# Transposing every second expert block by DMA in place of every third, and seeding before the transposing transfer is issued

## The reference

```python
# layer 1: masked linear
w_masked = weight * elem_mask            # 32x32 blocks of the mask
x = x + layernorm(x) @ w_masked.T
# layer 2: mixture of experts, 8 experts, top 2
h = layernorm(x)
_, top_idx = top_k(h @ W_gate + b_gate, 2)
y_all = relu(einsum('bsd,edh->bseh', h, W_e) + b_e)
x = x + take_along_axis(y_all, top_idx[..., None], axis=2).mean(axis=2)
```

## Time and profile before

| what | value |
|---|---|
| time, median of 3 runs | 684.41 us (682.28 to 686.14) |
| the profiled execution's own time | 682.73 us |
| its span in the profile | 681.0 us |
| PE busy | 661.3 us (97%) |
| DVE, ACT, POOL busy | 300.6, 338.0, 274.5 us (44%, 50%, 40%) |
| granted TensorE clock | 0.996 |
| experts' stage | from about 245 us to the end |

### The profile page before, as it was taken

One profiled execution on the slowest core, in us unless ns is written; L12 is line 12 of the kernel. 1 busy time (PEld: TensorE's weight loads), 2 busy tenths in 40 slices (PEclk: granted clock), 3 DMA queues, 4 the chain that ended last, 5 costly groups with the idle time before them and its releaser, 6 DMA issues.

```text
span 681.0 us, 11115 instructions
## 1 busy us (share of the span) xinstructions
PE 661.3 (97%) x3455; PEld 537.2 (79%) x3455; DVE 300.6 (44%) x559; ACT 338.0 (50%) x437; POOL 274.5 (40%) x254
## 2 busy tenths in 40 slices
PE   6999999999999999999999999999999999999993
PEld 4667777878888787888887888888888888888883
DVE  5886688887796645351440640441542420000000
ACT  6876855678784435343443435353535353535340
POOL 2023121235382454445362635362636353535231
PEclk9999999999999999999999999999999999999998
DMA  8991946699773499688699795787795966342423
GB/s 346 408 407 43 375 186 224 240 324 321 253 247 155 172 247 255 164 246 205 176 275 120 201 265 124 181 248 159 200 281 133 231 184 111 45 83 37 89 37 56
DMA packets 62165, 137.08 MB, mean 201 GB/s; under 512 B 30240, under 2 KB 30240, under 8 KB 62112
## 3 DMA queue, kind: packets, MB, share of 16 engines
q1 hardware_dynamic: 25776, 92.85, 37.7%
q0 software_dynamic: 11376, 37.23, 25.8%
q10 hardware_dynamic: 24960, 6.29, 6.3%
HBM read 87.59 MB, written 46.14 MB: 196 GB/s over the span
## 4 chain that ended last, share of the span: by engine, by line
PE 91%; DMA 3%; ACTq 1%; DVE 1%; ACT 1%; issue 1%; SPq 0%; POOLq 0%; POOL 0%
PE psO L491 80%; PE psT L781 3%; PE psT L491 2%; PE psT L524 2%; PE psO L524 1%; PE psG L597 1%; DMA xb<-data_t 1%; DMA x<-x_planes,tok_of 1%; DMA raw<-L_ffn_W_e 1%; ACTq L1096 1%; PE psS L578 1%; DVE slots L1397 1%; PE psT L565 0%; PE psT L609 0%; DVE slots L1395 0%
## 5 line engine op out<-in xcount | busy, mean ns | idle before, releaser
L491 PE MATMUL psO<-slots,xT 128*128 (+1 forms) x1872 | 432.8, 391 | 1.9 <-ACT psO L1056 1.5
L491 PEld LDWEIGHTS psO<-slots,xT 128*128 128x128 f32 x1872 | 349.2, 188 | 74.0 <-issue 2.6
L491 PE MATMUL psO<-wT,xT 128*128 128x512 f32 x624 | 152.3, 397 | 0.0
L1759 POOL DMA_INDIRECT rows_out<-xb,tok_of x36 | 61.1, 1697 | 209.4 <-ACT xb L1143 205.3
L1395 DVE CAST slots<-raw 128x1024 fp32r<-128x1024 f32 x56 | 56.6, 1010 | 190.3 <-PE psO L491 99.3
L1143 ACT ACTIVATE xb<-psO 128x512 f32<-128x512 f32 x78 | 46.6, 598 | 182.4 <-PE psO L491 182.4
L491 PEld LDWEIGHTS psO<-wT,xT 128*128 128x128 f32 x624 | 114.3, 188 | 25.1 <-issue 2.7
L1753 POOL TENSOR_TENSOR xT<-x2T,xT 128x1024 fp32r<-128x1024 f32 x38 | 94.6, 2490 | 16.6 <-ACT x2T L1119 14.4
L1056 ACT ACTIVATE psO<-bias_slot 128x512 f32 (+1 forms) x78 | 47.0, 602 | 76.9 <-issue 36.1
L1397 DVE TENSOR_TENSOR slots<-raw,slots 128x1024 fp32r<-128x1024 f32 x56 | 68.6, 1225 | 1.9
L1681 POOL TENSOR_SCALAR rs<-squares 128x1 f32<-128x1 f32 x16 | 8.8, 551 | 70.5 <-ACT rows_a L905 41.1
(11 more groups left out here) (238 smaller groups left out, 563.3 us busy)
## 6 DMA issues: line engine op xcount, KB each, us to landing
raw<-L_ffn_W_e SPq DMA_DIRECT2D x56, 512.0 KB, 5.1
x_rows<-x SPq DMA_DIRECT2D x16, 512.0 KB, 4.6
xb<-data_t SPq DMA_DIRECT2D x12, 512.0 KB, 4.3
mask_stage<-mask_blocks SPq DMA_DIRECT2D x8, 512.0 KB, 11.4
w_stage<-weight_t SPq DMA_DIRECT2D x8, 512.0 KB, 12.2
row_stage<-L_attn_weight SPq DMA_DIRECT2D x8, 512.0 KB, 10.7
xr<-L_attn_data SPq DMA_DIRECT2D x8, 512.0 KB, 5.8
x_planes<-planes_even SPq DMA_DIRECT2D x8, 512.0 KB, 3.0
```

The source lines that it names most:

```text
L491: last = eng.matmul(psum, xT[:, p, a, kt, :], moving(b, kt), start=(i == 0 and kt == 0 and not seeded), stop=(i == len(PASSES) - 1 and kt ...
L1759: eng.indirect_dma_start(out, bass.IndirectOffsetOnAxis(ap=tok_col(b), axis=0), xb[:, b % 2, :], None, bounds_check=N_TOK + P - 1, compute ...
```

## The change

Blocks 5, 7, ..., 37 go the DMA way (17 in place of 12), so `rows_of`, the gathers, POOL's order and ACT's joins follow from `by_dma`. On ACT the seed of half 0 of block b + 1 (with its two value loads) comes ahead of `turn_rows(b + 3)`; and a turn now waits for the join of the block two before it in place of three. DVE's table of how many turns must have landed ahead of a pair of weight loads is computed anew: a turn every four counts of `c_half` in place of every six, and never a turn that is issued behind the seed of the block for which those weights are wanted (`through - 2`); that takes four more small instructions.

```diff
@@ -315,7 +315,7 @@
         GATHER_AT = NB - 2
 
         def by_dma(b):
-            return b > EARLY + 2 and b % 3 == 2
+            return b > EARLY + 2 and b % 2 == 1
 
         def turns_of_pe(b):
             return len([c for c in range(1, b + 1) if not by_dma(c)])
@@ -324,7 +324,7 @@
             return len([c for c in range(1, b + 1) if by_dma(c)])
 
         N_TURNS = turns_of_dma(N_BLOCKS - 1)
-        assert [b for b in range(N_BLOCKS) if by_dma(b)] == list(range(5, 5 + 3 * N_TURNS, 3))
+        assert [b for b in range(N_BLOCKS) if by_dma(b)] == list(range(5, 5 + 2 * N_TURNS, 2))
 
         def turn_bank(b):
             return 0 if b == 0 else (b + 1) % 2
@@ -468,7 +468,7 @@
                     if kt % 2 == 0 and n > KT:
                         pair = n // 2 - 1
                         if n == KT + 2:
-                            eng.wait_ge(c_pace, KT // 2 + 4)
+                            eng.wait_ge(c_pace, KT + 4)
                         turned_by = after_turn[0:1, pair % (KT // 2), pair // (KT // 2) - 1:pair // (KT // 2)]
                         eng.wait_ge(l_turn, eng.value_load(turned_by, min_val=16, max_val=16 * (N_TURNS + 1)))
                     eng.dma_start(raw[:, kt % 2, :], w_rows(expert, kt)).then_inc(l_raw[kt % 2], 16)
@@ -1092,7 +1092,7 @@
                     eng.wait_ge(l_x1[2], 16 * uses_of(2, NB))
                     eng.wait_ge(c_ln2, NB)
                 else:
-                    eng.wait_ge(c_rhi, 2 * (b - 3))
+                    eng.wait_ge(c_rhi, 2 * (b - 2))
                 eng.dma_start_transpose(turned[:], rows_of(b).bitcast(U16)).then_inc(l_turn, 16)
 
             def join_rows(b):
@@ -1142,12 +1142,12 @@
                     eng.wait_ge(c_half, NH * (b + 1) + n + 1)
                     eng.activation(xb[:, b % 2, n * HALF:(n + 1) * HALF], psO[:, n, :], ACT.Relu,
                                    scale=1.0 / TOP_K).then_inc(c_out, 1)
-                    if n == 0 and b + 3 < N_BLOCKS and by_dma(b + 3):
-                        turn_rows(b + 3)
                     if b + 1 < N_BLOCKS:
                         if n == 0:
                             slot = biases_of(b + 1)
                         seed_half(b + 1, slot, n)
+                    if n == 0 and b + 3 < N_BLOCKS and by_dma(b + 3):
+                        turn_rows(b + 3)
                     if b == 1 and n == 0:
                         rows_hi(b + 1)
 
@@ -1615,12 +1615,16 @@
                 eng.scalar_tensor_tensor(pace[:, j, :], through[:, 0:N_EXP - 1], float(j), through[:, 1:N_EXP],
                                          ALU.add, ALU.min).then_inc(c_pace, 1)
             eng.wait_ge(c_pace, KT // 2)
-            eng.tensor_scalar(turn_part[:], pace[:], -1.0, 43.0, ALU.add, ALU.mult).then_inc(c_pace, 1)
-            eng.wait_ge(c_pace, KT // 2 + 1)
-            eng.tensor_scalar(turn_no[:], turn_part[:], 8, None, ALU.logical_shift_right).then_inc(c_pace, 1)
-            eng.wait_ge(c_pace, KT // 2 + 2)
+            for j in range(KT // 2):
+                eng.scalar_tensor_tensor(turn_no[:, j, :], through[:, 1:N_EXP], -2.0, pace[:, j, :],
+                                         ALU.add, ALU.min).then_inc(c_pace, 1)
+            eng.wait_ge(c_pace, KT)
+            eng.tensor_scalar(turn_part[:], turn_no[:], -3.0, None, ALU.add).then_inc(c_pace, 1)
+            eng.wait_ge(c_pace, KT + 1)
+            eng.tensor_scalar(turn_no[:], turn_part[:], 2, None, ALU.logical_shift_right).then_inc(c_pace, 1)
+            eng.wait_ge(c_pace, KT + 2)
             eng.tensor_scalar(turn_part[:], turn_no[:], float(N_TURNS), 1.0, ALU.min, ALU.add).then_inc(c_pace, 1)
-            eng.wait_ge(c_pace, KT // 2 + 3)
+            eng.wait_ge(c_pace, KT + 3)
             eng.tensor_scalar(after_turn[:], turn_part[:], 16.0, None, ALU.mult).then_inc(c_pace, 1)
             for e in range(2, N_EXP):
                 for kt in range(KT):
```

## The result

| | before | changed |
|---|---|---|
| median of 5 runs | 682.71 us (682.28 to 686.14) | 675.64 us (674.96 to 675.84) |
| span of the profiled execution | 681.0 us | 673.9 us |
| turns by DMA / by PE | 12 / 27 | 17 / 22 |

The ratio is 0.9885 (95% interval 0.9861 to 0.9908): 1.15% faster, where 0.94% was forecast. The medians differ by 7.07 us, which is 1.04%. Timed again (experiment 5), the changed kernel had 675.69 us beside 683.52, ratio 0.9881 (0.9863 to 0.9898).

A forecast was written before the change was run, and what follows sets the result against it. PE was taken to bound the kernel, so savings of 4.5 us (five fewer PE turns) and 1.9 us (seed gaps) summed to 6.4, from the 684.41 us median to 678.0 us, 0.9% faster; range 675.0 to 682.5 us.

The forecast's parts named there:

- part 2: Seed put ahead of the turn's issue on ACT: PE's three gaps vanish, 1.01 + 0.42 + 0.51 = 1.9 us saved.
- anchor: Starting time for the savings: median of three runs, 684.41 us, giving 678.0; the profiled execution, 682.73, gives 676.3.
- What bounds the kernel: PE, 97% busy over the 681.0 us span and 308.62 of 308.70 us in nearly the whole expert stage.
- part 1: Five blocks fewer turned by PE, 0.89 us each: 4.5 us saved, all on the path.
- The swap has to be there: With denser turns PE wants the seed about 4.6 us after the evacuation; the old order reaches 4.6 to 5.9.
- Part 3: Single buffers for gathered planes and turned rows, round 34.4 to 22.7 us: cost nothing, bounds 0 and 30 us.
- rival B: Late planes or a stretched turn hold ACT in two or three of 16 rounds: 680 to 683 us; chance 0.13.
- Rival C: The buffers' round bounds: denser turns and other transfers slow one another, 1.9 us per round, 708 us; chance 0.06.
- The 65% of the DMA engines: DMA engines' busy share in the expert-stage stretch, given as evidence against transfers slowing one another until the round bounds.
- Part 4: SP's holds of weight loads until turns land: three of 2.8 us don't reach the 16.22 us cover; cost nothing.
- 1309 ns for a tile by DMA: The skill's table, 390 ns on TensorE: as an estimate 20.9 us a turn and a loss; the trace's 5 us disagreed.

The follow-up runs named there:

- experiment 5: The changed kernel timed again with nothing altered, beside the kernel before: 675.69 us against 683.52.
- experiment 1: Kernel before with only the seed moved ahead of the turn's issue, plus the limit on weight-load holds this needs; turns every third block as before: 679.21 us, ratio 0.9947.
- Experiment 2: Changed kernel (every second block by DMA) with the old order, the turn's issue ahead of the seed: 684.93 us, ratio 1.0015.
- experiment 6: Changed kernel with two buffers each for gathered planes and turned rows, and two in place of three for the PE way: 675.2 us.
- f2: Changed kernel with two buffers of each kind and every block from 5 on turned by DMA (34 turns): 699.83 us, ratio 1.0207.
- experiment 4: Changed kernel without SP's wait for turns ahead of a pair of weight loads: 675.39 us, ratio 0.9891.
- g2: Changed kernel with SP holding a pair of weight loads already when the next turn is due within one half block: 674.93 us, ratio 0.9889.
- experiment 9: Changed kernel with two buffers of each kind and a dense tail, every block from 30 on turned by DMA: 670.22 us, ratio 0.9818.

## Why the prediction was right in kind, and what was off in size

The step that failed is the price of part 2. A late seed was priced at the matmul side's gaps, 1.9 us, and it cost what the weight-load side stood idle, 2.67 us. The median came out 2.4 us below the forecast, 675.64 and not 678.0; 1.7 of that are the anchor (below), and the 0.8 of this step account for the rest.

- **What bounds the kernel, and part 1**: right. The stretch from block 0 to block 38 lost 7.22 us, of which 2.67 are the order's (experiment 1), so 4.55 are the five turns, 0.91 each; the term was 4.5, with 0.89 each from a bare block rounded to 10.9 (it is 10.88).
- **Part 2** is the term that was mis-sized: 1.9 us, by adding up PE's idle brackets. By the periods between evacuations it cost 2.67. The list I read had the line for PEld, 2.6 us in three times, and I took the matmul side. Experiment 2 has the same at a longer stall: PE's gap is 2.54 us, the weight-load side's 2.77, and the block took 14.57 us in place of 11.79, 2.78 more. Why the two sides differ by a quarter of a microsecond isn't shown; the ends of matmuls are modelled in these profiles, so it may lie in the record of PE's gap.
- **The anchor** made it 678.0 rather than 676.3. The profiled execution (682.73) with the measured terms gives 682.73 - 7.2 = 675.5, and 675.64 came out; the median of the first three runs, 684.41, stood 1.7 above what five runs gave. That part of the miss is scatter.
- **The swap has to be there** (part 2's last sentences): right. Alone the denser turns gave nothing, 684.93 us. In the sum 4.5 and 1.9 stand as two gains, but the 4.5 come only with the swap.
- **Part 3** took the worst turn of one trace, 15 us, as the worst there is. 21 us came in an unchanged kernel, and 28 beside the first loads. Its verdict for the median, nothing, was right (experiment 6); rival B comes in 1 of the 11 runs of the changed kernel and costs 4 us, by one stall and not by two or three.
- **Rival C** was not this change's, but it starts not far behind: f2. The time is decided by single turns that meet other traffic and not by the mean round. The 65% of the DMA engines that stood against it was a mean over two stages: in the kernel before they are at 0.80 from 257 to 550 us, while weights are loaded, and at 0.42 behind, and the change made the first 0.88.
- **Part 4**: right about the cost of the holds (experiment 4), but not about their size. It took three of 2.8 us at most; the changed kernel has 29.4 us in six, the longest 8.4. The cover was real: the 47.8 us of holds in g2 cost PE 1.2 us, at one place.
- **The Trainium skill's** 1309 ns for a tile by DMA ("VectorE: DVE Perf Modes", "The three transpose paths") made 20.9 us of a turn. The trace disagrees for a turn by itself: 16 tiles land in 4.3 us. That a stretched one took just 20.9 us is chance, since others took 13 to 28. Its rule to turn 128x128 tiles on TensorE where PSUM will do ("Rules for kernel authors") did not pay here, where TensorE bounds the kernel: each block turned by DMA instead saved 0.91 us.

Left open: why the runs of the kernel before differ by 3 us (there is one profile of it), and what makes the worst turns: the weight loads, the bias's load, the gathers and adds, or the order of descriptors. No run takes one of them away alone. The fastest version is the dense tail, 670.22 us, with the reserve that two of its seven runs were slow.

## What to carry to other kernels

Where an engine's queue both feeds the bounding engine and issues slow transfers, put the feed first; moving work off the bounding engine pays only while what it waits for stays ahead. Price a stall by the period that it lengthens; here that was the weight-load side's gap and not the matmuls'. Read a share of busy time by stages. Before making a transfer more frequent, look for the longest one in several executions and at what was in flight beside it, and make it dense where that other traffic has ended.

## What the runs showed of the hardware that I had not expected

- **A transposing transfer and others in flight together can slow all of them.** By itself a turn's 2080 packets pass in 2.6 to 2.9 us and it lands 4.3 us after its issue (changed kernel, experiments 5 and 9). In experiment 5, beside a 512 KB load (usually 5.2 us), the bias's load, an add and a gather, all took 16 to 21 us, at 129 GB/s over all queues. Meeting a load isn't enough for it: in the kernel before, the turn issued at 459.41 had 1.05 MB of plain loads beside it, and all its packets passed within 459.5 to 467.2 us. Nor is a load needed: the packets of the 14.0 us turn of experiment 9 took 10.6 us with only gathers and adds beside them. Loads alone came as far (10.2 us for the turn issued at 343.10 in experiment 4). All thirteen turns whose packets took over 12 us, in the fourteen traces, had both kinds beside them.
- **A stall of PE can cost twice, or not.** After the 1.83 us stall of experiment 5, behind a PE that had been busy throughout, the granted clock fell. The windows of that execution, with the clock in the third column from the end:

```profile
414.00:420.00 6.00, 6.00 (x31) 4.90 (x28) 0.00 (x0) 0.00 (x0) 2.35 (x1) 1.00 1.07 197
420.00:422.20 2.20, 0.37 (x3) 0.01 (x1) 0.00 (x0) 1.34 (x3) 0.00 (x0) 1.00 1.07 199
422.20:424.00 1.80, 1.80 (x5) 1.50 (x6) 0.00 (x0) 1.80 (x3) 1.56 (x2) 0.64 0.00 1
424.00:426.00 2.00, 2.00 (x6) 1.55 (x5) 0.00 (x0) 1.00 (x2) 2.00 (x1) 0.50 0.96 96
428.00:432.00 4.00, 4.00 (x19) 3.31 (x18) 2.38 (x3) 2.29 (x3) 1.88 (x2) 1.00 0.82 242
```

  At 0.5 (1.2 of 2.4 GHz) a matmul takes 632 ns in place of 391. That block took 14.48 us in place of 10.88: 3.6 lost, of which the weight-load side's idle time is 2.25. The stalls of 0.4 to 1.0 us in the kernel before left the clock at 1.00. So did a longer one, of 2.54 us, in the trace of experiment 2, also behind a busy PE:

```profile
545.00:555.08 10.08, 10.08 (x49) 8.23 (x47) 2.03 (x3) 3.79 (x3) 4.59 (x2) 1.00 0.98 215
555.08:557.60 2.52, 0.00 (x1) 0.00 (x0) 1.81 (x2) 0.83 (x2) 0.00 (x0) 1.00 0.78 158
557.60:562.00 4.40, 4.38 (x19) 3.69 (x20) 0.00 (x0) 2.75 (x4) 2.71 (x2) 1.00 0.31 29
```

  It cost no more than the 2.78 us told above. So the length of the stall doesn't decide alone whether the clock falls; what does is not shown.
